# A graph layer with experts on one core: 20 dense edge sets in place of 12, and another split of the gathers over its stages

## What is computed

```python
def reference(x, src, dst, L0_gnn_W, L0_gnn_b, L0_mix_Wqkv, L0_mix_Wout, L0_mix_gamma, ...):
    edge_index = jnp.stack([src, dst])
    xn = _layernorm(x, axis=-1)
    x = x + _L0_gnn_ref(xn, edge_index, L0_gnn_W, L0_gnn_b) \
          + _L0_mix_ref(xn[None], L0_mix_Wqkv, L0_mix_Wout, L0_mix_gamma)[0]
    x = x + _L0_ffn_ref(_layernorm(x, axis=-1)[None], ...)[0]
    return x
```

## Time and profile before

| what | value |
|---|---|
| median of 3 runs | 1843.76 us (1841.33 to 1844.39) |
| span of the profiled execution, its only time on the page | 2433.1 us |
| PE busy | 1851.1 us, 76% of the span |
| weight loads busy | 1449.7 us, 60% |
| DVE busy | 1222.2 us, 50% |
| ACT busy | 685.0 us, 28% |
| POOL busy | 1277.6 us, 53% |
| gathers | 1299, mean 978 ns busy |
| mean granted PE clock | 0.908 |

### The profile page before, as it was taken

The page is one execution under the profiler, slowest core; times in us unless marked ns, Lnnn a source line. Parts: engine busy times, 40 slices in busy tenths (PEclk is TensorE's granted clock), DMA queues, the critical chain, the costliest instruction groups (busy, mean ns, idle before and its releaser), DMA issues.

```text
span 2433.1 us, 34393 instructions
## 1 busy us (share of the span) xinstructions
PE 1851.1 (76%) x11044; PEld 1449.7 (60%) x11044; DVE 1222.2 (50%) x4533; ACT 685.0 (28%) x1736; POOL 1277.6 (53%) x1310
## 2 busy tenths in 40 slices
PE   0578877878748787787887787877778777777888
PEld 0355555666526665666666666666666666666677
DVE  8322222442235555455555555555555555555576
ACT  6333333332202222222222222222222222222233
POOL 1655565464655654655555555655555555545510
PEclk9899999998868988988989998988998989988999
DMA  7445554443642332322332332332332322322310
GB/s 256 140 147 158 161 158 142 121 118 106 183 120 79 98 94 66 100 77 85 98 89 80 90 94 83 94 89 76 91 92 84 90 85 85 90 81 84 92 42 13
DMA packets 144715, 251.14 MB, mean 103 GB/s; under 512 B 28046, under 2 KB 96062, under 8 KB 144542
## 3 DMA queue, kind: packets, MB, share of 16 engines
q0 software_dynamic: 62352, 170.35, 24.6%
q1 hardware_dynamic: 82190, 78.59, 10.1%
HBM read 216.74 MB, written 32.09 MB: 102 GB/s over the span
## 4 chain that ended last, share of the span: by engine, by line
PE 47%; another core or an unknown queue 22%; DVE 11%; issue 11%; ACT 8%; DMA 1%; SPq 1%; POOL 0%; DVEq 0%; POOLq 0%; ACTq 0%
PE ps_hidden L867 9%; PE ps_expert L878 9%; PE ps_zone L653 3%; PE ps_zone L655 3%; PE ps_proj L832 3%; PE ps_proj L805 2%; PE ps_proj L835 2%; ACT sb_stage L1039 2%; PE ps_zone L697 2%; PE ps_turned L662 2%; PE ps_zone L699 2%; PE ps_hidden L761 2%; PE ps_proj L761 2%; PE ps_expert L687 1%
## 5 line engine op out<-in xcount | busy, mean ns | idle before, releaser
L609 POOL DMA_INDIRECT sb_ring<-xn_table,sb_idx x1299 | 1270.1, 978 | 1050.4 <-PE ps_zone L655 485.3
L878 PE MATMUL ps_expert<-sb_arena,sb_stage 128*128 128x256 f32 x1568 | 444.7, 408 | 61.4 <-DVE sb_arena L1531 34.0
L1039 ACT ACTIVATE sb_stage<-ps_hidden,sb_b_col 128x128 f32<-128x128 f32 x784 | 241.7, 365 | 874.3 <-remote 469.1
L867 PE MATMUL ps_hidden<-sb_arena 128*128 128x128 f32 x3136 | 458.5, 293 | 27.7 <-ACT sb_stage L1039 21.0
L867 PEld LDWEIGHTS ps_hidden<-sb_arena 128*128 128x128 f32 x3136 | 415.8, 206 | 64.6 <-issue 30.7
L1531 DVE SCALAR_TENSOR_TENSOR sb_arena<-ps_expert,sb_small,sb_arena 128x256 f32<-128x256 f32 x392 | 189.0, 482 | 337.1 <-remote 211.6
L653 PE MATMUL ps_zone<-sb_ring,sb_onehot 128*128 128x256 f16 x1299 | 336.6, 287 | 22.6 <-issue 12.4
L878 PEld LDWEIGHTS ps_expert<-sb_arena,sb_stage 128*128 128x128 f32 x1568 | 287.4, 204 | 99.5 <-issue 58.3
L655 PE MATMUL ps_zone<-sb_ring,sb_onehot 128*128 128x257 f16 x1299 | 337.1, 288 | 6.2 <-issue 6.2
L655 PEld LDWEIGHTS ps_zone<-sb_ring,sb_onehot 128*128 128x128 f16 x1299 | 133.5, 103 | 62.6 <-issue 19.3
L653 PEld LDWEIGHTS ps_zone<-sb_ring,sb_onehot 128*128 128x128 f16 x1299 | 134.6, 104 | 51.5 <-issue 14.5
(11 more groups left out here) (175 smaller groups left out, 2267.8 us busy)
## 6 DMA issues: line engine op xcount, KB each, us to landing
sb_ring<-xn_table,sb_idx POOLq DMA_INDIRECT x1299
keys_values<-sb_stage SPq DMA_DIRECT2D x49, 256.0 KB
sb_stage<-keys_values SPq DMA_DIRECT2D x96, 128.0 KB
sb_sums<-x SPq DMA_DIRECT2D x7, 896.0 KB, 11.1
sb_stage<-x SPq DMA_DIRECT2D x49, 128.0 KB
xn_transposed<-sb_stage SPq DMA_DIRECT2D x49, 128.0 KB
sb_arena<-xn_transposed SPq DMA_DIRECT2D x49, 128.0 KB
sb_arena<-x SPq DMA_DIRECT2D x49, 128.0 KB
```

The lines of the kernel that those rows point to most:

```text
L609: pool.indirect_dma_start(ring3[:, place, 0:2 * D], None, table, bass.IndirectOffsetOnAxis(tile_idx, 0)).then_inc(signal, 16)
L867: mm = pe.matmul(hidden[e % 2][:, j * P:(j + 1) * P], w1_sb[:, e, c, j * P:(j + 1) * P], halves(tokens_t[b % 2])[:, c, :], start=c == 0, s ...
L878: mm = pe.matmul(expert[e % 2][:, 0:D], halves(act_h[e % len(act_h)])[:, c, :], w2_sb[:, e, c, :], start=c == 0, stop=c == KC - 1, skip_gr ...
L1039: ins = act.activation(halves(act_h[e % len(act_h)])[:, j, :], hidden[e % 2][:, j * P:(j + 1) * P], ACT.Gelu, bias=b1_col[:, e * KC + j:e ...
```

## The change

The number of dense sets goes from 12 to 20, so that 440 tiles instead of 264 are summed from dense sets, and 1123 instead of 1299 are gathered. A unit of the first pass has 5 gathered tiles instead of 4, of the second 4 instead of 3, and the dense budgets rise to 3.8 and 4.2 from 2.1 and 2.7. The passes then hold 441 gathered tiles in place of 343, and the last stage 666 in place of 940, at 1.9 a step in place of 2.6; its last tile comes in step 353. The last dense set ends in unit 36 of the second pass, as before. In the first pass ACT copies a finished zone ahead of the block's keys and values instead of behind them. The one-hot ring has 20 places instead of 16. To make room, some tensors of the start-up part share memory with others, and the ones in the ring's last 10 slots (6 before) are written later. The changed file has three more lines ahead of the functions, so line numbers are 3 higher there, and 4 from the key copy on.

```diff
-SETS = 12
+SETS = 20
...
-OH_RING = 16
+OH_RING = 20
...
-B1_TILES, B2_TILES = 4, 3
-B1_DENSE, B2_DENSE = 2.1, 2.7
+B1_TILES, B2_TILES = 5, 4
+B1_DENSE, B2_DENSE = 3.8, 4.2
 BUILD_COST, HI_COST, FINISH_COST = 0.46, 0.23, 0.6
 HEAD0_TILES = (4, 4, 8)
-MAIN_RATE = 2.6
+MAIN_RATE = 1.9
...
-        stats = [sb("stats0", 6 * GROUP_MOST), sb("stats1", 6 * GROUP_MOST)]
...
+        stats = [key_onehot[:, :].bitcast(F32)[:, TILES + n * 6 * GROUP_MOST:TILES + (n + 1) * 6 * GROUP_MOST]
+                 for n in (0, 1)]
         row_number, row_float = set_sb[0:1, 0:GROUP_SPAN], set_sb[0:1, GROUP_SPAN:2 * GROUP_SPAN]
-        PLACE_SLOT = RING - 6
+        PLACE_SLOT = RING - 10
...
-        group_rel, group_out, src_hi, src_lo = (
-            before_adj[:, TILES + n * DENSE_TILES:TILES + (n + 1) * DENSE_TILES] for n in range(4))
+        group_rel, group_out = (
+            before_adj[:, TILES + n * DENSE_TILES:TILES + (n + 1) * DENSE_TILES] for n in range(2))
+        after_place = ring[:, PLACE_SLOT * (2 * D + 1):RING * (2 * D + 1)].bitcast(F32)
+        src_hi, src_lo = (after_place[:, n * DENSE_TILES:(n + 1) * DENSE_TILES] for n in range(2))
...
                 dense(u.before)
+                copy_zones(u.tiles)
                 act.wait_ge(kv_filled, b + 1)
                 wait(act, kv_stored[b % 2], b // 2 * 16)
                 wait(act, k_maxed, b)
                 act.activation(kv_b[b % 2], kv_bank[b % 2][:, :], ACT.Copy).then_inc(kv_copied, 1)
-                copy_zones(u.tiles)
                 dense(u.after)
...
             dve.wait_ge(turn_filled, USE["place"] + 1)
-            dve.memset(ring3[:, PLACE_SLOT:RING, 2 * D:2 * D + 1], 1.0).then_inc(cleared, 1)
             dve.tensor_copy(shifted16[:, :], cst[:, 0:3 * P])
...
             dve.wait_ge(idx_landed, 16)
+            dve.wait_ge(turn_filled, USE["place"] + 1)
...
             dve.wait_ge(edge_chain, 4)
+            dve.memset(ring3[:, PLACE_SLOT:RING, 2 * D:2 * D + 1], 1.0).then_inc(cleared, 1)
```

## The result

Four runs of the changed kernel have a median of 1988.04 us (1980.40 to 1994.15), four of the kernel before 1843.26. The ratio is 1.079 (95% interval 1.076 to 1.082). The change makes the kernel 7.9% slower; 3.7% were predicted, and the measured time lies 13 us above the upper end of the range, 1975.

What follows compares the result with a forecast made beforehand. PE and POOL were almost equal before, POOL leading by a hair; after the change PE sets the passes and last stage. 68 + 645 + 15 (heads) + 1063 + 112 + 8 = 1911, taken as 1912 us; range 1842 to 1975.

Steps and rivals of the forecast that it cites:

- POOL leads by a hair: Last stage before the change: a block with gathers takes 25.4 us on PE against 26.0 on POOL.
- The sum before: Whole kernel before the change: 67 + 465 + 20 + 1188 + 80 + 8 = 1828 us, 16 short of 1844.
- the leftover: The 16 us missing from the sum before, taken for coupling between PE and POOL and not carried over.
- PE's waits in the passes: Both passes: build runs wait for ACT's evictions, 24 us before and 44 after; zone and turn waits were priced separately.
- zone copies inside a unit: Passes: 24 zones end inside a unit and PE waits 0.64 us each for ACT's copy, 15 us, before 4.
- turns behind DVE's add: Passes: turning and adding zones costs PE a little wait as before, 16 us against 17.
- waits for gathers at the end of the second pass: Last 12 or 13 units without dense work: PE needs 18 us, the gathers some 38, so 20 more.
- -93 in the last stage: Last stage: blocks of 24.1 us with gathers, then 22.83 without, 1175 us against 1268, 93 less.
- -16 of coupling: Whole kernel: the 16 us of PE and POOL coupling vanish, as one is no longer close behind in the last stage.
- the passes did not stay with the gathers: Denies the rival that PE's waits fall into gather waits: passes 593 us, kernel 1828, chance 0.14.
- the last stage did follow: Denies the rival that an ACT and DVE chain keeps last-stage blocks at 26.1 us: kernel 1999, chance 0.06.
- long runs are paced by DVE: Rival, passes: build runs over two unit halves cost 2 to 2.5 us more each; passes 690, kernel 1956, chance 0.2.

Runs made afterwards that it cites:

- two other kernels with 15.2 and 20.8 tiles: Builds alternating with gathered tiles on PE and ACT: in the changed kernel (15.2 tiles) 1953.4 us; with 12 sets and the numbers of before (20.8 tiles) 1840.0 us.

## Why the prediction was right in sign and half in size

*What bounds.* Right, and closer than it said. The two engines are nearly equal before, in the passes as in the last stage. But from "POOL leads by a hair" in the last stage it drew too much. The block's pitch against its gathered tiles, from the table: 15.2 tiles 24.59, 17.4 tiles 24.83, 17.9 tiles 24.94, 18.6 tiles 25.04, 19.0 tiles 25.18, 20.1 tiles 25.25, and then 20.8 tiles 25.90 (two other kernels with 15.2 and 20.8 tiles have 24.71 and 25.85, which shows the scatter). Up to 20.1 a tile costs (25.25 - 24.59) / 4.9 = 0.13 us; the last 0.7 tiles cost 0.65. So in the last stage the gathers bind only above some 20 tiles, and only by half a microsecond a block. That is why eight sets more gave so little back there.

*The base.* The sum before had 465 us for the passes and 16 left over. Undisturbed, the passes take 485: 343 gathers at 1.25 plus the 25 of slow ones are 454, as in the prediction, POOL waits 24 more for PE, and the last context product comes 6 us behind the issue of the 343rd gather. Most of the 24 are two waits, behind the turn from the first pass to the second and at 507 us:

```profile
368.41 1.28 POOL L609 DMA_INDIRECT sb_ring<-xn_table,sb_idx  x1 [11.35 <-PE ps_zone L655]
...
507.32 0.94 POOL L609 DMA_INDIRECT sb_ring<-xn_table,sb_idx  x1 [5.75 <-PE ps_zone L655]
```

From the last context product to the last stage's first router product the trace has 31 us where the sum had 20, and from there to the end 1259 where the sum had 1276. So the leftover stood ahead of the last stage and not in it. The prediction let the change gain it, since it had put it down to PE and POOL close together in the last stage; nothing of it was gained.

*PE's waits in the passes.* The mechanisms that were priced are there, one size was off. Forecast and tallied: builds 44 and 64, zone copies inside a unit 15 and 16, turns behind DVE's add 16 and 16 or a little more, waits for gathers at the end of the second pass 20 and about 20. With smaller ones, some 17 us that the forecast had at nothing, all waits are some 133 us where the forecast had 95, and PE's work, forecast at 552, is some 550: together the 683 us from the first gather at 69.6 to the last context product at 752.8. (In the kernel before, zone copies were 16 us too and not 4, 13 of them in two waits near the end of the second pass, while POOL issued on without a pause.) The build waits by the length of a run as PE executed it, each from the run's first build to the next instruction of another kind, less 0.115 us a matmul:

| groups in the run | runs | us each | forecast |
|---|---|---|---|
| 1 | 21 | 0.24 | nothing |
| 2 | 15 | 0.78 | 0.5 |
| 3 | 21 | 0.80 | 0.65 |
| 4 | 10 | 1.12 | 0.8 |
| 5 | 1 | 1.45 | 1.2 |
| 6 and 7 | 9 | 1.86 | none counted |

Of the 19 us above the forecast some 11 are runs of two to five that cost more than their price (the run of four shown above, 0.85, is cheaper than their mean), 5 are single groups, and 3 are runs of six and seven. These arise in the second pass, where one unit's last builds join the next unit's first; the forecast counted each half of a unit by itself. The zone's price is the 0.75 us of the earlier trace rows, at the changed kernel's ACT copy too (230.29 to 231.04). Passes after: 686 to the last context product, 41 more than forecast, against 20 more before: 21 of the miss. The way from there to the last stage took 42 us, before 43; 5 less were forecast. In that stretch the granted clock was 0.78, before 0.86 (the windows above), which may be the reason and was not tried.

*Last stage.* A block without gathers has 22.83 us in the changed kernel too (1889.38 to 1912.21 and on to 1935.04), as in the earlier trace rows. The changed kernel's blocks are 1.3 us shorter than before, not 2. With 15.2 tiles I had 24.1; it is 24.59: by the prediction's own sum 15.2 tiles fill 1.8 us of the slack and not 2.3, while 20.1 tiles fill 2.3 (22.83 + 4.46 + 0.3 - 25.25). It had taken 2.3 for any number of tiles. 44.1 x 0.49 = 22 us. And the kernel before has 25.90 and not 26.1, 45.5 x 0.2 = 9 us. With the 16 of coupling these are 47, and the stage missed by 46. **This is the step that failed:** "-93 in the last stage" (a block of 24.1 with 2.3 us of slack filled) and "-16 of coupling" (a leftover given to the change without a row that showed where it stood) are -63 together. The passes and the way to the last stage, +200 for +176, are the other 24 us: the change's passes took 41 us more than forecast, 20 of build waits and some 17 of smaller ones, and the kernel before took 20 more. That PE would end last, and behind what, was right; these sizes were not, and the leftover had no mechanism behind it.

The rivals: the passes did not stay with the gathers, and the last stage did follow. Of the second, *long runs are paced by DVE*, the number came out (690 us, and the passes took 686), but that is luck: its mechanism is there, at a third of its size. A run of seven groups, over two unit halves:

```profile
636.32 0.39 PE L690 MATMUL ps_expert<-sb_key_onehot,sb_lo_onehot 128*128 128x264 f16 x2
...
639.34 0.63 PE L690 MATMUL ps_expert<-sb_key_onehot,sb_lo_onehot 128*128 128x264 f16 x4 [0.44 <-DVE sb_key_onehot L1275]
...
640.92 0.40 PE L690 MATMUL ps_expert<-sb_key_onehot,sb_lo_onehot 128*128 128x264 f16 x2 [0.26 <-DVE sb_key_onehot L1275]
...
641.39 0.27 PE L656 MATMUL ps_zone<-sb_ring,sb_onehot 128*128 128x256 f16 x1
```

The wait for DVE comes behind four groups, the lead that the rival named. But there are nine such runs at 1.86 us, 17 us, where it had all 20 sets at 2 to 2.5. In builds of the two passes PE stood idle 16.6 us for ACT's evictions and 9.8 for DVE's key one-hot. In the trace's waits of the first pass, behind the first line (26.4 us, ahead of the first gather):

```profile
...
PE ps_turned L665 <- DVE sb_sums L1367: 13.0, 15, 2.2
PE ps_expert L690 <- ACT sb_adjacency L982: 10.2, 25, 0.6
PE ps_zone L656 <- ACT sb_zone_sb L971: 5.9, 12, 0.7
PE ps_hidden L690 <- ACT sb_adjacency L982: 3.5, 8, 0.6
PE ps_hidden L690 <- DVE sb_key_onehot L1275: 2.7, 4, 2.1
```

These idle times are shorter than what the pitches lose, since matmuls overlap and a wait costs that overlap as well: in the run shown first, two matmuls take 0.70 us, 224.61 to 225.31, for 0.23 of work, with 0.31 idle. Given by pitch to what ended the idle time, the build waits are some 30 us for ACT, 12 to 14 for DVE and 20 where no idle time of 0.15 us or more shows. What the smaller waits are has not been separated.

In one sentence: a set takes 16.6 us of PE and gives back 22 gathered tiles, worth 0.22 us of PE each in the passes' work and 0.13 in the last stage's blocks, 3 to 5 us; it pays only against gathers that bind, and with 16 and with 20 sets it did not pay in any arrangement tried. Fewer than 12 sets were not tried.

## What to carry to other kernels

Where two engines came out within a few per cent of each other, the time was above both sums (the passes before: 454 and, by the forecast, 441 us against a measured 485), and relief for either ended at the other after a few microseconds: price a trade by both, and count no slack of the one as room without adding work to it on the chip. Count runs of like work as the engine executes them, over the borders of the program's units. Before moving work off an engine that seems to bind, change the rate at which it is fed by a few per cent: the kink in the block's pitch (0.13 us a tile below 20.1 tiles, nearly 1 above) showed a gain of 22 us that needed no other edit. A leftover of a sum belongs to the stage where it is found; if the trace can't say where, it must stay on both sides of the comparison.

## What the chip showed that I had not expected

The pauses of the earlier trace rows were in none of the other traces. The same kernel spanned 2433.1 us in the first and 1841.1 in the second profile, while the gather's pitch (1.25 us) and the block without gathers (22.83 us) were the same in both. What the pauses are is open; pitches from stretches between them could be trusted, means over whole stages could not. And a gather slows by 30% (0.957 to 1.240 us) beside a comparison of 128x2160 float16, in the same trace; with builds and tiles interleaved at 12 sets the mean beside it is 1.37 us, and 1.27 in the same kernel without.
